# Two heads to one product: 64 rows by 128 columns of TensorE for q, k and the mix, in place of two products of 64 by 64

## The reference, cut to what matters

```python
def _proj(W, b, x):                      # W is 64 x 64, over the 64 rows of a batch item
    return jnp.einsum('oi,bil->bol', W, x) + b[:, None]
q = _proj(Wq, bq, layernorm(x)); k = _proj(Wk, bk, ctx); v = _proj(Wv, bv, ctx)
# 8 heads of 64 of the 512 channels; B = 32 batch items, D = 64 rows
scores = jnp.einsum('hbdk,hbek->hbde', qh, kh) * scale
p = softmax(scores)
xh = jnp.einsum('hbde,hbek->hbdk', p, vh)
x = x + _proj(Wo, bo, xh)                # back in [b, d, l]
# then x + FFN(layernorm(x)): gate and up 512 -> 1792, silu(gate) * up, down 1792 -> 512,
# the weights dequantized as (integer - zero) * scale, in groups of 128 rows
```

## Time and profile before

| | |
|---|---|
| median of 3 runs | 435.25 us (434.01 to 436.29) |
| the profiled execution | 434.57 us, span in the trace 432.8 us |
| PE busy | 410.4 us, 95% |
| PEld busy | 317.9 us, 73% |
| DVE, ACT, POOL busy | 330.4, 330.5, 265.8 us |
| granted clock of TensorE, mean | 0.996 |

### The profile page before, as it was taken

One profiled execution on the slowest core, in us unless ns is written; L12 is line 12 of the kernel. 1 busy time (PEld: TensorE's weight loads), 2 busy tenths in 40 slices (PEclk: granted clock), 3 DMA queues, 4 the chain that ended last, 5 costly groups with the idle time before them and its releaser, 6 DMA issues.

```text
span 432.8 us, 10751 instructions
## 1 busy us (share of the span) xinstructions
PE 410.4 (95%) x4228; PEld 317.9 (73%) x4228; DVE 330.4 (76%) x582; ACT 330.5 (76%) x540; POOL 265.8 (61%) x264
## 2 busy tenths in 40 slices
PE   7878988999988999999999999999999999999994
PEld 5655666777856777777777878677877888888872
DVE  4778666998878778788887777787887667667676
ACT  2438898897877788687778888687888998988970
POOL 3335797899588654665473954755566555555561
PEclk9899999999999999999999999999999999999999
DMA  7677746966742000002010000000000000001003
GB/s 255 190 230 259 279 147 226 300 204 209 241 121 69 2 11 16 26 2 76 12 39 26 2 0 27 27 2 26 26 27 0 2 1 9 17 24 50 1 1 97
DMA packets 26792, 35.44 MB, mean 82 GB/s; under 512 B 1870, under 2 KB 18422, under 8 KB 26742
## 3 DMA queue, kind: packets, MB, share of 16 engines
q1 hardware_dynamic: 26434, 34.71, 24.5%
q10 hardware_dynamic: 244, 0.05, 0.1%
q0 software_dynamic: 64, 0.00, 0.0%
HBM read 30.56 MB, written 4.19 MB: 80 GB/s over the span
## 4 chain that ended last, share of the span: by engine, by line
PE 73%; DVE 9%; issue 6%; POOL 6%; ACT 4%; DMA 1%; POOLq 0%; SPq 0%; DVEq 0%; ACTq 0%
PE banks L764 20%; PE banks L766 19%; PE banks L777 10%; PE banks L778 9%; PE banks L663 4%; DVE yT L1039 2%; PE banks L703 2%; ACT banks L555 2%; PE banks L692 2%; PE banks L673 2%; PE banks L681 2%; POOL t_sb L416 1%; DVE st L925 1%; PE banks L722 1%; DVE qkT L943 1%
## 5 line engine op out<-in xcount | busy, mean ns | idle before, releaser
L555 ACT ACTIVATE banks<-banks,ratio 128x512 f32<-128x512 f32 x336 | 207.8, 664 | 34.9 <-PE banks L766 25.4
L1039 DVE SCALAR_TENSOR_TENSOR yT<-banks,sd,yT 128x512 f32<-128x512 f32 x208 | 154.1, 746 | 48.8 <-PE banks L778 48.1
L764 PE MATMUL banks<-xT,wgu 128*128 128x512 f32 x448 | 182.2, 407 | 5.2 <-DVE t_sb L1024 2.5
L766 PE MATMUL banks<-xT,wgu 128*128 128x512 f32 x448 | 175.1, 391 | 0.0
L416 POOL TENSOR_TENSOR t_sb<-t_sb,u_sb 128x512 f32<-128x512 f32 x56 | 72.7, 1298 | 63.1 <-DVE t_sb L1024 63.0
L764 PEld LDWEIGHTS banks<-xT,wgu 128*128 128x128 f32 x448 | 84.1, 188 | 27.6 <-issue 3.7
L766 PEld LDWEIGHTS banks<-xT,wgu 128*128 128x128 f32 x448 | 84.3, 188 | 15.2
L777 PE MATMUL banks<-hr,wd 128*128 128x512 f32 x224 | 89.3, 399 | 4.2 <-DVE yT L1039 2.3
L778 PE MATMUL banks<-hr,wd 128*128 128x512 f32 x224 | 87.5, 390 | 0.0
L429 POOL TENSOR_TENSOR hr<-t_sb,hr 128x512 fp32r<-128x512 f32 x56 | 73.1, 1305 | 5.1 <-ACT hr L577 0.7
L777 PEld LDWEIGHTS banks<-hr,wd 128*128 128x128 f32 x224 | 42.0, 188 | 19.3 <-DVE yT L1039 9.5
(11 more groups left out here) (93 smaller groups left out, 383.9 us busy)
## 6 DMA issues: line engine op xcount, KB each, us to landing
x_sb<-in_x SPq DMA_DIRECT2D x16, 256.0 KB, 5.2
out<-x_sb SPq DMA_DIRECT2D x16, 256.0 KB, 2.1
wgu_in<-in_L_ffn_gate_w SPq DMA_DIRECT2D x7, 512.0 KB, 5.7
z_in<-in_L_ffn_gate_z SPq DMA_DIRECT2D x7, 512.0 KB, 5.4
wgu_in<-in_L_ffn_up_w SPq DMA_DIRECT2D x7, 512.0 KB, 5.5
z_in<-in_L_ffn_up_z SPq DMA_DIRECT2D x7, 512.0 KB, 5.0
wd_in<-in_L_ffn_down_w SPq DMA_DIRECT2D x7, 512.0 KB, 5.3
z_in<-in_L_ffn_down_z SPq DMA_DIRECT2D x7, 512.0 KB, 4.6
```

The source lines that it names most:

```text
L555: act.activation(banks[:, bank, :], banks[:, bank, :], ACT.Copy, scale=ratio[:, m, g, it:it + 1]).then_inc(done[n % 2], 1)
L764: pe.matmul(banks[:, bank, :], w, xT[:, c % 2, 0, g, :], start=g == 0, stop=False, skip_group_check=True)
L766: pe.matmul(banks[:, bank, :], w, xT[:, c % 2, 1, g, :], start=False, stop=True, skip_group_check=True).then_inc(full[n % 2], 1)
L1039: dve.scalar_tensor_tensor(y, bank, sd[:, it, b:b + 1], y, ALU.mult, ALU.add).then_inc(s_free, 1)
```

## The change

`project` and `mix` take two heads as one stationary operand of 128 columns; the result then fills all 128 partitions of the bank, where two products filled 64 each. For `mix`, the two heads j and j + 4 have to lie side by side in `e_sb`, so `score` writes its blocks in another order (0, 2, 1, 3). `values`, `apply`, all other engines' instructions and all waits stay as they are.

```diff
@@ project
-                        for b, hp in TURNS:
-                            r, k = HALVES[b], HALVES[hp]
-                            h = 2 * c + hp
-                            mm = pe.matmul(banks[k, at + b, (m * NC + c) * D:(m * NC + c + 1) * D],
-                                           src[r, h * Lh:(h + 1) * Lh], wT[r, m, :], start=True, stop=True)
+                        for b, r in enumerate(HALVES):
+                            mm = pe.matmul(banks[:, at + b, (m * NC + c) * D:(m * NC + c + 1) * D],
+                                           src[r, 2 * c * Lh:2 * (c + 1) * Lh], wT[r, m, :], start=True, stop=True)
@@ score
-                        mm = pe.matmul(banks[o, at + hp, c * D:(c + 1) * D], qkT[r, b, c * D:(c + 1) * D],
+                        to = 2 * (c % 2) + c // 2
+                        mm = pe.matmul(banks[o, at + hp, to * D:(to + 1) * D], qkT[r, b, c * D:(c + 1) * D],
@@ mix
-                    for b, g in TURNS:
-                        r, o = HALVES[b], HALVES[g]
-                        h = NC * g + j
-                        mm = pe.matmul(banks[o, 6 + b, j * D:(j + 1) * D], e_sb[r, t % 2, h % 2, h // 2, :], wT[r, 3, :],
-                                       start=True, stop=True)
+                    for b, r in enumerate(HALVES):
+                        mm = pe.matmul(banks[:, 6 + b, j * D:(j + 1) * D], e_sb[r, t % 2, j % 2, 2 * (j // 2):2 * (j // 2) + 2, :].rearrange("p g e -> p (g e)"),
+                                       wT[r, 3, :], start=True, stop=True)
```

## The result

The changed kernel takes 460.4 us (median of four runs, 457.3 to 464.6), the one before 434.6 beside it: 1.056 times as long, 95% interval 1.047 to 1.065. Slower, as forecast, by 26 us where 20 were forecast; the median lies 0.4 us beyond the upper end of the range, 447 to 460. The profiled execution took 464.6 us, 30 more than that of before, and is the longest of the four.

What follows compares the result with a forecast made beforehand. TensorE was taken to set the pace from 45 us on, a chain of waits before that. Terms 9.5 + 5.2 + 1.3 + 6.4 - 1.9 = +20.5 on 434.57 us gave 455 us, range 447 to 460.

Steps and rivals of the forecast that it cites:

- what sets a step: In `project` and `mix` bursts, the weight load sets the step; with 128 columns it grows from 58 to 112 ns.
- the one-column products of L827: Quarters loading 64 columns but streaming 1 still take 55 ns a step, so the load alone is enough.
- The pace unchanged: Rival: `project` and `mix` steps stay at 58 ns, only switches and first loads are new; 436 us, chance 0.06.
- the cost per instruction: Rival: each instruction costs 14.6 ns, so 768 fewer make the kernel faster, about 424 us; chance 0.04.
- the loads taking turns: Rival: loads in the two halves take turns, a step is 214 ns; about 495 us, chance 0.04.
- the new switch: From `apply` to `mix` in MA bursts, the array's split changes: 0.14 us each, 1.3 us for 9 bursts.
- what is absorbed: In the loop, PE's waits on other engines shrink by the work put ahead of them: -1.9 us.
- the waits of 1.16 and 1.14 us: PE waits at 56.74 and 69.79 for ScalarE and GpSimd's chain; to absorb a QK (0.86) and an M (0.43).
- the one of 0.85: PE's wait at 123.06, to absorb an M with its switch (0.57 us).
- the start: Ahead of the loop, longer projections and mixes, the first at half pace, add 6.9 less 0.5, +6.4 us.
- a gap of 1.07 us: Ahead of the loop, a gap put down to issue alone; halved instructions may shorten it, so 0.5 us taken off.
- a step of 118 ns: Range term: a step of 118 in place of 112 if the second half's turn is not hidden, +2.2 us.

Runs made afterwards that it cites:

- mix_only: Only `mix` changed (with the order in which `score` writes), everywhere, `project` as in the kernel before: 440.7 us, 1.014 times the kernel before.
- the seven groups: Seven groups of identity products in quarters, halves and full array, put behind the last product of the kernel before to time a step; run once, 459.7 us.
- start_only: Two heads to a product only ahead of the loop, the loop as in the kernel before: 449.2 us, 1.029 times the kernel before.
- bench: The kernel before with seven groups of identity products behind its last product, nothing of the output left out; run once, 459.7 us.
- whole: The changed kernel run again as it is, on the same chip as its variant with a filling block: 463.5 us, 1.064 times the kernel before.

## Why the prediction came out as it did

**Right: what sets a step.** The forecast was 112 ns, from 188 against 135 ns of load and the one-column products of L827. It is 112 at L927 and in the bursts; `project` costs +0.84 us (forecast 0.86) and `mix` +0.41 (0.43; mix_only and the trace of after: 1.36 us from the product ahead to the one behind in place of 0.94). The pace unchanged, the cost per instruction and the loads taking turns are all refuted by the rows of the seven groups.

**Right: the new switch.** Forecast 0.14; an MA burst grew by 0.57 and an M burst by 0.41, so 0.16. Some 0.10 of it is the longer way from `apply` to `mix`, 0.15 in place of 0.05.

**Right as a sum, not place by place: what is absorbed.** The second chunk grew by 5.45 (forecast 5.6), the first, with as many bursts, by 3.6. So some 1.9 us of it were absorbed, the forecast's number; PE's idle time in that chunk went from 7.3 to 5.3 us. But the waits of 1.16 and 1.14 us shrank by 0.93 each, where 0.86 and 0.43 were forecast, the one of 0.85 is gone, and a wait of 0.91 stands where there was none:

```profile
71.67 0.47 PE L763 MATMUL banks<-xT,wgu 128*128 128x512 f32 x1 [0.23 <-DVE t_sb L1023]
...
84.67 0.47 PE L763 MATMUL banks<-xT,wgu 128*128 128x512 f32 x1 [0.21 <-DVE t_sb L1023]
...
102.00 0.47 PE L763 MATMUL banks<-xT,wgu 128*128 128x512 f32 x1 [0.91 <-DVE t_sb L1023]
```

That the sum fits is in part luck. In all the loop was forecast at 9.5 + 5.2 + 1.3 - 1.9 = 14.1 and has 13.6.

**Wrong: the start.** The step that failed is "The first ones run at half pace (...), so the first grows by 1.7; the second begins later and may by then be at full pace": the moment at which TensorE reaches full pace was taken as fixed. The sum for the start was +6.4, with +1.5 as its upper bound's part; it measured +15.3 in the profiled execution and +14.0 to +14.3 in the two others of the same kernel. I took the moments at which TensorE changes its level from the trace of before and let only the loads grow. But the level followed what TensorE did, and the change altered just that: with halves whose load is longer than their stream, the lower level stayed until 45 to 48 us in three profiles, and until 32.1 in start_only's. Every product, also those of `score`, `apply` and `stir`, which the change doesn't touch, cost nearly double for that long. With the streams doubled and nothing else, the start is +2.8. So of some 14 us, about 3 are loads and about 11 the level, an estimate from these two starts (48.3 and 59.4 to 59.7). That the streams are what mattered is shown for the start as a whole; which of its bursts kept the level down is not, nor why the same products ahead of the loop had the upper level from 32.1 us once and from 45 to 48 three times. The 0.5 that the sum took off for a gap of 1.07 us had no ground either: bench, whose products ahead of the loop are those of the kernel before, has no such gap within its `score`. The range took the first products at either pace, but no start that remains at the lower one; that case was missing among the rivals. That the time lies at the edge of the range nonetheless is luck: the room above the forecast was there for other terms, a step of 118 ns and less absorbed, and what the start cost beyond its bound took it up.

## What to carry to other kernels

Count a small product on TensorE as the longer of load and stream of its part of the array: twice the columns in a stationary operand of the same use of the array are no saving if the stream is shorter than the load, and halving the instructions is worth nothing while they aren't what sets the step. Four quarters with 64 columns loaded and 64 streamed were balanced; two halves with 128 loaded and 64 streamed were not. And before the clock is up, price a change at both levels, and ask whether it will still rise where it rose before.

## What the hardware showed that was not expected

- TensorE can have busy records without a gap for 21.3 us and stay at 1.2 GHz all the while (windows of "whole"); with twice the columns streamed in the same products it was at 2.4 GHz from 10.7 us. The Trainium skill has the level set by how busy the engine has been ("TensorE: Matmul & The Clock Gate", "What's actually happening"); by these rows, the busy time that a profile shows isn't the measure of that.
- Work that nobody reads can pay: a block of filling products, 4.2 us of it, came with 3.9 us less in all, doubled streams with 7.3 to 9.5.
- A granted clock of 1.00 at the beginning of a profile may mean only that no change was recorded yet: the first profile of the changed kernel shows 1.00 while its steps take 0.22 us.
